# Thirty-six of 782 scatters moved from one program of GpSimd into the two before it

## The reference, cut to what matters

```
layer 0:  m_e = sigmoid([h_src,h_dst] a_t + c_t) * (relu([h_src,h_dst] W1_t + b1_t) W2_t + b2_t)   (t = edge type, 4 of them)
          agg[dst] += m_e ; a GRU of agg and h, plus h, layer norm
layer 1:  attention over edge_index[0] (rows = src), neighbours edge_index[1] (cols = dst)
layer 2:  64 relations over 8 bases, times edge weight, summed by dst, plus a root term, relu
layer 3:  three graph convolutions over the same edges, then + x
```

## Time and profile before

| | us |
|---|---|
| median of 3 runs | 8862.63 (8857.88 to 8871.75) |
| the profiled execution, its own time | 8860.16 |
| its span | 8858.3 |
| GpSimd busy | 6250.7 (71%) |
| TensorE, VectorE, ScalarE busy | 5186.5, 5017.0, 2419.6 |
| the 782 scatters by targets (line 523), first to last start | 175.7 to 1211.3 |
| the 784 gathers of the first pass (line 909) | 1226.6 to 2207.1 |
| the 782 scatters by sources (line 1102) | 2236.1 to 3286.8 |

### The profile page before, as it was taken

How to read it: one execution, slowest core, us unless ns; L and a number is a source line. 1 busy time by engine, 2 the same in 40 slices (tenths; PEclk the granted TensorE clock), 3 DMA queues, 4 the chain that set the end, 5 groups by cost and what they waited for, 6 DMA issues and landing times. The chain is left out here.

```text
span 8858.3 us, 139803 instructions
## 1 busy us (share of the span) xinstructions
PE 5186.5 (59%) x33091; PEld 4364.7 (49%) x33091; DVE 5017.0 (57%) x16146; ACT 2419.6 (27%) x7480; POOL 6250.7 (71%) x6393
## 2 busy tenths in 40 slices
PE   7657537899782006555589999834444444444443
PEld 4326427788541005444469999833333333333333
DVE  9988725666665006666668888843333333333334
ACT  0001014445011006767658888700000000000000
POOL 2777777777678767777537777577776777767776
PEclk9977769999676557787699999955555555555555
DMA  1001112222101002222379999722222212121112
GB/s 40 3 6 36 32 37 55 55 55 54 21 8 31 1 12 54 53 53 53 42 293 386 380 382 390 281 55 52 53 53 59 53 52 53 52 59 52 52 52 60
DMA packets 387376, 789.79 MB, mean 89 GB/s; under 512 B 162523, under 2 KB 199197, under 8 KB 386574
## 3 DMA queue, kind: packets, MB, share of 16 engines
q0 software_dynamic: 296832, 702.37, 25.9%
q1 hardware_dynamic: 89806, 81.61, 2.8%
q10 hardware_dynamic: 320, 0.80, 0.0%
HBM read 717.69 MB, written 66.66 MB: 89 GB/s over the span
## 5 line engine op out<-in xcount | busy, mean ns | idle before, releaser
L2045 POOL DMA_INDIRECT edge_rows<-tab,all_slots x2352 | 2259.7, 961 | 876.0 <-issue 715.9
L2095 PE MATMUL edge_psum<-edge_rows,edge_onehot 128*128 x4992 | 1262.8, 435 | 1746.6 <-DVE edge_onehot L2065 1486.3
L2095 PEld LDWEIGHTS edge_psum<-edge_rows,edge_onehot 128*128 128x128 f32 x4992 | 1094.5, 324 | 1914.6 <-issue 1914.5
L2075 DVE TENSOR_TENSOR acc_acc<-acc_acc,edge_psum 128x128 f32 x2496 | 716.1, 287 | 1866.0 <-PE edge_psum L2095 1594.3
L181 POOL DMA_INDIRECT edge_rows<-tab,acc_pair_src x832 | 824.1, 990 | 499.3 <-issue 214.5
L1851 PE MATMUL edge_p_m<-edge_rows,edge_onehot 128*128 128x128 f32 x9984 | 1126.0, 276 | 38.5 <-ACT edge_rows L1783 34.6
L1851 PEld LDWEIGHTS edge_p_m<-edge_rows,edge_onehot 128*128 128x128 f32 x9984 | 1119.8, 192 | 44.7 <-issue 29.0
L523 POOL DMA_INDIRECT slots_d<-all_slots,pro_row_d x782 | 788.8, 1009 | 401.4 <-issue 247.4
L1783 ACT ACTIVATE edge_rows<-edge_rows,edge_coef 128x128 f32<-128x128 f32 x3328 | 995.4, 387 | 162.5 <-DMA edge_rows<-tab,acc_pair_src 162.5
L181 POOL DMA_INDIRECT edge_rows<-tab,edge_slots x832 | 809.8, 973 | 270.3 <-issue 253.2
L1102 POOL DMA_INDIRECT slots_s<-acc_pays,acc_row_s x782 | 805.1, 1030 | 274.6 <-issue 246.5
(11 more groups left out here) (406 smaller groups left out, 9057.0 us busy)
## 6 DMA issues: line engine op xcount, KB each, us to landing
edge_rows<-tab,all_slots POOLq DMA_INDIRECT x2352, 2.5
tab<-tab_o SPq DMA_DIRECT2D x50, 512.0 KB, 2.6
edge_rows<-tab,edge_slots POOLq DMA_INDIRECT x832, 2.6
edge_rows<-tab,acc_pair_src POOLq DMA_INDIRECT x832, 5.8
tab_src<-all_x SPq DMA_DIRECT2D x50, 260.0 KB, 2.0
all_x<-tab_src,all_slots POOLq DMA_INDIRECT x784
slots_d<-all_slots,pro_row_d POOLq DMA_INDIRECT x782
slots_s<-acc_pays,acc_row_s POOLq DMA_INDIRECT x782, 2.1
```

The lines of the kernel that those rows point to most:

```text
L2045: pool.indirect_dma_start(out=rows[:, (g % R3) * G + j, :], out_offset=None, in_=D[f"tab3_{layer}"][:, :], in_offset=bass.IndirectOffsetOn ...
L2075: v.tensor_tensor(at, at, psum[:, slot % 2, j * P:(j + 1) * P], ALU.add).then_inc(q["added"], 1)
L2095: m = pe.matmul(psum[:, slot % 2, j * P:(j + 1) * P], onehot[:, slot % 2, j, :], flat(rows[:, ds(values[j], 1), :]), start=True, stop=True)
```

## The change

The loop of scatters by sources becomes a helper with a range of columns, and is cut in three. Columns 0 to 11 are scattered in the prologue's program of GpSimd, behind the last scatter by targets, with two waits ahead of them: for `pays` and for the first 16 columns of `row_s`. Columns 12 to 35 are scattered in the first pass' program, behind the last gather. Columns 36 to 781 stay in the middle. No instruction but the two waits is added, and none is removed.

```diff
+EARLY, EARLIER = 36, 12
...
+def scatter_by_source(pool, K, D, first, last):
+
+    for c in range(first, last):
+        pool.indirect_dma_start(out=D["slots_s"][:, :], out_offset=bass.IndirectOffsetOnAxis(ap=K["row_s"][:, c:c + 1], axis=0),
+                                in_=K["pays"][:, c, :], in_offset=None).then_inc(K["scattered"][2 + c % 2], 16)
...
 (prologue, gpsimd, behind the loop of scatters by targets)
+            pool.wait_ge(q["paid_s"], 1)
+            pool.wait_ge(q["rows_s"], 1)
+            scatter_by_source(pool, K, D, 0, EARLIER)
...
 (edges0, gpsimd, behind the loop of gathers)
+            scatter_by_source(pool, K, D, EARLIER, EARLY)
...
 (middle, gpsimd)
-            for c in range(EC):
-                pool.indirect_dma_start(out=D["slots_s"][:, :], out_offset=bass.IndirectOffsetOnAxis(ap=K["row_s"][:, c:c + 1], axis=0),
-                                        in_=K["pays"][:, c, :], in_offset=None).then_inc(K["scattered"][2 + c % 2], 16)
+            scatter_by_source(pool, K, D, EARLY, EC)
```

## The result

The changed kernel takes **8835.44 us** (median of 9 runs, 8827.84 to 8844.97) against 8862.64 for the kernel before on the same chip (9 runs). The ratio is 0.9969, 95% interval [0.9959, 0.9979]: 27 us faster. Forecast was 8844.4 us, that is 18.3 us faster. The direction held, and the gain is half as large again; 8835.4 lies about halfway between the forecast (8844.4) and what rival A would give (8826). The profiled execution has a span of 8829.8 us, 28.5 less than before.

What follows compares the result with a forecast made beforehand. GpSimd's scatters and gathers were taken to bound all three stages. Middle -45.4, prologue +14.1 and first pass +13.0 sum to -18.3 us, so 8862.63 becomes 8844.4 us; range 8836 to 8853, or 8833 to 8858 with part of the rivals.

Steps and rivals of the forecast that it cites:

- rival A: Prologue and first pass ends: GpSimd's DRAIN tail runs beside the added scatters; -36.4 us in all, 8826; chance 0.09.
- The middle ends with its scatters, at 1.261 us each: Middle: GpSimd's scatters end it, so 36 fewer at 1.261 us start to start give -45.4 us.
- The rival price, the mean of 1.345: Middle: each scatter costs the whole group's mean, so 36 fewer give 48.4 us; no chance of its own.
- Rival C: Middle: long VectorE instructions hold GpSimd longer, losing 22 us (8866) or 54 us (8899); chance 0.04.
- GpSimd's DRAIN goes on behind its last DMA and is exposed in all three stages: Prologue, first pass and middle ends: DRAIN lasts 9.05 us past the last scatter, so idle gaps hold fewer scatters.
- First pass +13.0: First pass end: 24 scatters (30.3 us) and a 9.05 us tail end it at 2247.4, not 2234.4.
- Rival B: First pass end: the DRAIN tail is 14.1 us as in `edges1`, stage +18.1; -13.2 us in all, 8849; chance 0.07.
- Prologue +14.1: Prologue end: 12 more scatters move GpSimd's DRAIN end from 1221.3 to 1236.4; the engines had met at 1222.3.
- The middle's tail stays 9.05: Middle end: GpSimd's DRAIN still ends last, 9.05 us after the last scatter, despite 36 fewer scatters.

Runs made afterwards that it cites:

- `late_drain`: Kernel before, plus a wait for SP's load of `slots_d` behind GpSimd's last prologue scatter; 11284 us, on a chip where the kernel before takes 11267.
- `pass36`: Against the kernel before: 12 scatters by sources in the prologue, 36 in the first pass, 734 left in the middle; 8847.68 us against 8875.34, ratio 0.9967.

## Why the prediction was right, and where it was mis-sized

- *The middle ends with its scatters, at 1.261 us each*: right. The rival price, the mean of 1.345, is out: from first to last start the middle got 46.2 us shorter (45.4 forecast, 48.4 by the mean), and the eight scatters held by VectorE add up to 58.4 us after and 58.6 before, with 36 scatters less. Rival C (VectorE holds GpSimd longer) is out with it.
- *GpSimd's DRAIN goes on behind its last DMA and is exposed in all three stages*: right, and the reason why 45.4 us taken from the middle don't come out as 45. Rival A (the tail runs beside what is added; 36.4 us) is out for the pass, which it has +3.9 us longer, and its mechanism is out by `late_drain`: the tail waits for the DRAIN. In the prologue its number came close all the same (+5.1 by A, +6.5 measured; without the 2.5 us by which all of it was early, the end lies at 1228.8, among the 1227 to 1232 that I gave as its sign), because the tail there is short for another reason.
- *First pass +13.0*: right to 0.1 us, but by luck, as two errors cancel. The tail there is 8.56 and not 9.05. I took it from the other stages; the number is that of the gathers' 6.60 and 24 x 0.082. Against these 0.5 us stand 0.3 by which the first gather starts later behind the meeting (4.65 us and not 4.32) and 0.2 in the scatters (30.46 us). Rival B (14.1 us) is out.
- *Prologue +14.1*: the term that was mis-sized most. Measured +6.5. I took the tail of 9.05 for a constant of scatters, since two stages had it. Both had 782 of them: it was one sample and not two. With 794 the block has passed number 785, the place of the next pause, and the tail is 1.7.
- *The middle's tail stays 9.05*: wrong by 2.9, for the same reason.
- With both terms put right: -45.4 - 2.9 + 6.5 + 13.0 = -28.8, against 28.5 in the trace and 27.2 in the medians. That the trace agrees so closely is in part luck: in it the prologue's 2.5 us less and the 3.7 us more behind the middle, which are not the change's, nearly cancel.

Beyond the cover (the 19.8 us by which GpSimd's DRAIN was over ahead of VectorE's) a scatter that is moved costs about as much in the pass as it saves in the middle. In the traces of `pass36` and the change 12 more moved cost 13.4 us there and save 12.0: nothing more is gained.

## What to carry to other kernels

A gap in which an engine stands idle at a stage's end is not room for work: ask on line 91's rows what that engine still does in its DRAIN, and who arrives last. For indirect scatters on GpSimd reckon with a tail that depends on how many stand in the block, here 0.082 us for each behind number 673 up to 782, and measure it anew when the block's count changes. And two samples of a duration are two only if they differ in what could set it.

## What the runs showed of the hardware that I had not expected

GpSimd's DRAIN outlasts the block's last indirect scatter by 0.13 us and 0.082 us for each scatter since the pause behind number 673 (5.13 us at 61 to 9.05 us at 109, where no other engine works). A pause comes every 112 scatters and shows as 1.70 us and not 0.30 between two scatters where nothing else delays it. Just around number 785 the tail is another (10.72 us at 784, 4.86 at 787, 1.71 at 794). Idle time does not serve for it: 456 us passed in `late_drain` without a start. Gathers leave some too, 6.6 to 6.8 us behind 784 of them, and show no pause of that kind; by what count was not tested. It is 6.6 us with 12 gathers outstanding and, in `late_drain`, with 4, so the tail is not the time of what is outstanding.

On two of the four chips of the experiments this kernel took 11170 and 11267 us, 26 to 27% longer than on the others, with GpSimd's pace unchanged at 1.26 us from one scatter to the next where it does not wait. The granted TensorE clock is lower there, 0.68 to 0.69 over the run and not 0.71 to 0.72, but in the ranking (180 to 600 us) TensorE and VectorE also do less: VectorE is busy for 154 of 420 us in `late_drain` and for 410 before, and waits 203 us for what the profile calls remote. On these chips the bound of the middle is another one, and what a change like this buys was not told from nothing. The cause of that state was not looked for.
